# Two decoder layers on one core: the weight loads of the second layer's self-attention are issued two steps later in each pair of heads

## The reference

```python
def _L1_attn_ref(x, w_q, w_k, w_v, w_o):
    q = jnp.einsum('bsd,hqd->bhsq', x, w_q)
    k = jnp.einsum('bsd,hqd->bhsq', x, w_k)
    v = jnp.einsum('bsd,hvd->bhsv', x, w_v)
    scores = jnp.einsum('bhsq,bhtq->bhst', q, k)
    causal = jnp.triu(jnp.ones((s, s), dtype=bool), k=1)
    masked = jnp.where(causal, -jnp.inf, scores)
    weights = jax.nn.softmax(masked / jnp.sqrt(jnp.float32(dq)), axis=-1)
    out = jnp.einsum('bhst,bhtv->bhsv', weights, v)
    cat = out.transpose(0, 2, 1, 3).reshape(b, s, -1)
    return jnp.einsum('bsf,df->bsd', cat, w_o)
```

## Time and profile before

| | before |
|---|---|
| median of 3 runs | 3018.79 us (3016.57 to 3022.42) |
| the profiled execution, its own time | 3010.78 us |
| its span, first to last instruction | 3008.8 us |
| mean granted TensorE clock | 0.867 of full speed |

### The profile page before, as it was taken

The page is one execution under the profiler, slowest core; times in us unless marked ns, Lnnn a source line. Parts: engine busy times, 40 slices in busy tenths (PEclk is TensorE's granted clock), DMA queues, the critical chain, the costliest instruction groups (busy, mean ns, idle before and its releaser), DMA issues.

```text
span 3008.8 us, 50636 instructions
## 1 busy us (share of the span) xinstructions
PE 2276.8 (76%) x17470; PEld 1830.6 (61%) x17470; DVE 2175.1 (72%) x4246; ACT 1060.2 (35%) x2004; POOL 585.9 (19%) x666
## 2 busy tenths in 40 slices
PE   3667788868776877886877687888677777888875
PEld 3556666657465756664755565666565566666663
DVE  6765788866866578885776667888586666788767
ACT  2312444422432244442242224444224223444324
POOL 2111222212101122221101112222120102222220
PEclk8778899989777889998877789999877878999988
DMA  6001689840001078983000119897100014899600
GB/s 234 1 15 40 137 160 171 154 86 1 1 15 56 15 149 161 170 152 63 1 1 15 56 37 167 166 164 144 31 1 15 1 55 85 161 169 166 113 1 14
DMA packets 658407, 251.39 MB, mean 84 GB/s; under 512 B 613082, under 2 KB 633946, under 8 KB 657370
## 3 DMA queue, kind: packets, MB, share of 16 engines
q1 hardware_dynamic: 653978, 243.79, 41.4%
q10 hardware_dynamic: 4160, 4.19, 0.4%
HBM read 52.87 MB, written 10.49 MB: 21 GB/s over the span
## 4 chain that ended last, share of the span: by engine, by line
issue 38%; PE 23%; DVE 18%; DMA 11%; ACT 5%; POOL 4%; DVEq 1%; ACTq 0%; SPq 0%; POOLq 0%
DMA l_ptb<-l_phb 6%; PE ps L233 5%; PE ps L235 5%; PE ps L234 4%; DMA l_pts<-l_phs 4%; DVE nmax L1385 3%; PE ps L1289 1%; DVE l_k L1440 1%; DVE l_q L1444 1%; DVE l_phb L1391 1%; DVE l_phs L1391 1%; ACT l_q L1351 1%; PE ps L1271 1%; ACT xn L1347 1%; POOL d_pn L990 1%
## 5 line engine op out<-in xcount | busy, mean ns | idle before, releaser
L1385 DVE TENSOR_REDUCE nmax<-ps 128x1 f32<-128x1024 f32 (+7 forms) x512 | 383.3, 750 | 23.0 <-PE ps L1273 20.9
L1494 POOL CAST l_phb<-l_pb 128x1024 f16<-128x1024 f32 (+3 forms) x256 | 241.4, 943 | 654.1 <-ACT l_pb L1336 337.8
L1336 ACT ACTIVATE l_pb<-ps,nmax 128x1024 f32<-128x1024 f32 (+3 forms) x256 | 244.7, 956 | 283.5 <-DVE nmax L1385 282.7
L1271 PE MATMUL ps<-l_k,l_q 128*128 128x512 f32 (+3 forms) x768 | 319.1, 416 | 24.3 <-ACT l_ps L1336 23.9
L1391 DVE TENSOR_TENSOR l_phb<-l_pb,l_phb 128x1024 f16<-128x1024 f32 (+3 forms) x256 | 288.2, 1126 | 15.5 <-POOL l_phb L1494 13.4
L1272 PE MATMUL ps<-l_k,l_q 128*128 128x512 f32 (+3 forms) x768 | 270.1, 363 | 0.0
L1289 PE MATMUL ps<-l_v,l_ptb 128*128 128x64 f16 x4992 | 197.8, 197 | 34.2 <-DMA l_ptb<-l_phb 34.1
L1289 PEld LDWEIGHTS ps<-l_v,l_ptb 128*128 128x128 f16 x4992 | 177.1, 101 | 67.4 <-DMA l_ptb<-l_phb 41.1
L233 PE MATMUL ps<-xTh,l_w 128*128 128x512 f32 x256 | 123.1, 481 | 83.9 <-DVE l_q L1444 50.5
L1494 POOL CAST l_phs<-l_ps 128x128 f16<-128x128 f32 (+3 forms) x256 | 124.2, 485 | 319.1 <-DMA l_pts<-l_phs 169.6
L1271 PEld LDWEIGHTS ps<-l_k,l_q 128*128 128x128 f32 x768 | 156.0, 203 | 44.2 <-ACT l_ps L1336 29.8
(11 more groups left out here) (361 smaller groups left out, 6279.4 us busy)
## 6 DMA issues: line engine op xcount, KB each, us to landing
l_k<-xn SPq DMA_DIRECT2D x128, 256.0 KB, 4.1
l_w<-l_wqk_s SPq DMA_DIRECT2D x32, 512.0 KB, 4.8
l_wv<-l_wv_s SPq DMA_DIRECT2D x16, 512.0 KB, 6.0
xin<-in_x SPq DMA_DIRECT2D x4, 1024.0 KB, 5.5
m_w<-in_m_w SPq DMA_DIRECT2D x8, 512.0 KB, 4.4
m_w<-in_m_w SPq DMA_DIRECT2D x4, 1024.0 KB, 9.2
l_wo<-in_l_wo SPq DMA_DIRECT2D x16, 256.0 KB, 4.5
l_ptb<-l_phb SPq DMA_TRANSPOSE x256, 4.1
```

The source lines that it names most:

```text
L1271: pe.matmul(s[:, c0:c1], q, L["l_k1"][:, h, c0:c1], start=True, stop=False)
L1336: s.activation(l_numer(k)[:, 0:n], l_banks(k)[:, 0:n], ACT.Exp, bias=nmax[:, k % 4:k % 4 + 1], accum_out=lsum[:, h, k % NT:k % NT + 1]).th ...
L1385: v.tensor_reduce(nmax[:, k % 4:k % 4 + 1], l_banks(k)[:, 0:n], AX.X, ALU.max, negate=True).then_inc(q_["max"], 1)
L1494: g.tensor_copy(l_parts(k)[:, 0:cols], l_numer(k)[:, 0:cols]).then_inc(q_["hi"], 1)
```

## The change

The three conditions `k == 2` in `l_sp` become `k == 4`. The loads stand behind the block of head 0's key copies in the program, so at k = 4 the order on SP is: transpose of step 8, the two key copies of head 0, the weight loads, transpose of step 9. No other engine's program changes. What is loaded, from where and into which buffers stays as it was.

```diff
                 if j + 1 < HP and k == 10:
                     l_dup(sp, b, j + 1, 1)
-                if j + 2 < HP and k == 2:
+                if j + 2 < HP and k == 4:
                     sp.wait_ge(*lower(b, ("Q", j + 1 - 1, 1)))
                     l_load_w(sp, b, j + 2)
-                if j % 2 == 0 and j + 2 < HP and k == 2:
+                if j % 2 == 0 and j + 2 < HP and k == 4:
                     sp.wait_ge(*lower(b, ("V", j // 2, 3)))
                     l_load_wv(sp, b, j // 2 + 1)
-                if j % 2 == 1 and j >= 3 and k == 2:
+                if j % 2 == 1 and j >= 3 and k == 4:
                     sp.wait_ge(*lower(b, ("O", j // 2 - 1, 3)))
                     l_load_wo(sp, b, j // 2)
```

## The result

| | before | after |
|---|---|---|
| median of 4 runs | 3017.68 us (3004.45 to 3022.42) | 3066.17 us (3056.75 to 3074.18) |
| ratio to before | | 1.0168 (95% interval 1.0133 to 1.0202) |
| span of the profiled execution | 3008.8 us | 3054.8 us |
| mean granted TensorE clock of that execution | 0.867 | 0.861 |

The change makes the kernel slower by 48.5 us, or 1.7%. Forecast were +43 us and 3062 us. Of the 46.0 us between the two profiled spans, 42.7 us lie in the self-attention: from the first to the last `l_pv` of a batch it takes 9.6, 14.1, 9.1 and 9.9 us more. The other 3.3 us I did not trace to a place.

A forecast was written before the change was run, and what follows sets the result against it. Bound by a loop through all engines; DMA work delaying step 9's transpose, less 1.5 us slack per pair, gives 12.2 us per batch, 49 us in four, less 6 us for first pairs: +43 us, 3062 us, range 3018 to 3104 us.

The forecast's parts named there:

- What bounds the kernel: Whole kernel: bound by the length of a loop through all engines, no single one full; PE busy 76%, DVE 72%.
- Hole: SP idle for 3.3 us before step 8's transpose; DMA share 0.80 to 1.06 with loads, 0.47 without.
- dense stretch: SP from step 8's transpose past step 15's: issues within about 0.5 us of each other, DMA share 0.96 to 1.02.
- Leaving the hole is worth nothing, but 1.6 us per batch: Step 7's transpose lands 3.7 us sooner, priced at nothing; only pair 0 gains, 1.6 us per batch.
- the sum that I gave back: Pair 0 of each batch: PE's waits at two transposes shortly after the loads vanish, 6 us in all.
- Who waits and for how much: Behind step 9's later transpose POOL's rounding, then DVE, wait; 1.5 us per pair absorbed, 1.1 to 2.9 us left.
- SP's issue runs beside the DMA work and is not added: Before step 9's transpose: load issues add 0.7 us each on SP, 1.4 us for two, beside the DMA work.
- the slack that I had read: POOL's 0.9 us after step 13's rounding plus DVE's idle 0.6 us: 1.5 us per pair absorbed.
- the row's price: Loads in the dense stretch: 1 MB costs 4.4 us by the trace, against 2.4 us by the skill's ceiling.
- Full price: Dense stretch: no slack, SP, DVE and DMA each near full; 60 to 85 us slower, about 3090 us; chance 0.22.
- Absorbed: Dense stretch: loads slip between transposes, only SP's 1.4 us issue remains; no change, 3013 to 3025 us; chance 0.10.
- faster: `l_pv` at steps 8 to 10: waits in all pairs echo the hole's loads; 19 us less, 3000 us; chance 0.13.

The follow-up runs named there:

- the copies at k = 12: Kernel before with head 1's key copies issued at k = 12 instead of 10, except for the last pair: 3037.9 us, ratio 1.0058.
- the one that moves everything: Kernel before with loads at k = 0, head 0's key copies at k = 3 and head 1's at k = 12: 3022.2 us, ratio 1.0012.

## Why the prediction was right

The place, the direction and the order of the waits were right. The size came out right in part by luck: the waits cost less than forecast, and the clock, for which the prediction had no term, added an estimated 11 to 13 us.

*What bounds the kernel.* Hole and dense stretch are there, and the runs with other steps show that they decide: from k = 0 to k = 3 the time changes by 6 us, and between 3 and 4 by about 48 us.

*Leaving the hole is worth nothing, but 1.6 us per batch.* With the work taken away and the issues left at k = 2, the kernel gained 6 us, the sum that I gave back, 4 us of it in pair 0. With the change, step 7's transpose of pair 4 landed in 3.2 instead of 5.6 us, and nobody used it. In pair 0, from step 4 to step 8 of PE, the change gained 0.95 us per batch, not 1.6 us.

*Who waits and for how much.* The place and the order were right: step 9's landing, POOL's rounding, DVE's remainder. Both sizes were off in opposite directions. For pair 4, mean of the four batches, step 9's transpose landed 3.4 us later, counted from the issue of step 8's (11.25 against 7.85 us), and not 4.0 to 4.4 us. Of this, 1.7 us are a later issue and 1.7 us a longer landing. PE's step from `l_pv` 8 to `l_pv` 9 grew by 2.6 us, so about 0.8 us was absorbed and not 1.5 us. One sign came out short: the landing was to take 6 us or more from its issue and took 5.5 us, since half of the delay came ahead of the issue.

The pairs, from the end of `l_pv` of step 4 to that of the next pair, mean of four batches, in us:

| pair | 0 | 1 | 2 | 3 | 4 | 5 | 6 |
|---|---|---|---|---|---|---|---|
| loads | w, wv | w | w, wv | w, wo | w, wv | w, wo | none |
| predicted | 1.3 | 1.1 | 2.9 | 1.2 | 2.9 | 1.2 | 0 |
| measured | 2.1 | 1.5 | 2.1 | 2.2 | 2.5 | 1.1 | -0.8 |
| added time at the lower clock | 4.3 | 2.6 | 2.6 | 2.6 | 1.7 | 1.7 | -1.7 |

The sums are 10.6 and 10.7 us per batch. That they agree so well is luck: the spread over pairs is flatter than the bytes say, and at 0.24 us for each us at the lower clock 3.3 of the 10.7 us go with the clock. About 7.4 us are left for what the prediction described.

*SP's issue runs beside the DMA work and is not added.* Half right. It is not added: the loads without an issue on SP cost 59 us (though from another queue and a little earlier), the issues alone 19.5 us and both together 48.5 us. With ACT's queue, step 9's transpose of pair 4 took 4.1 us longer to land (7.9 against 3.8 us, mean of four), which is the work that I had read from the hole (4.4 us); behind SP's issues 1.7 us of it were left. But I put the issues at nothing if alone, as 1.4 us against 1.5 us of slack. They cost 19.5 us, as the slack that I had read belongs to step 9, and the one that SP's delay hits is step 10. This may be what flattens the table above, since a small load adds nearly an issue's time whatever it carries; no run shows it pair by pair.

*The figure of the Trainium skill.* By the ceiling of 435 GB/s (the Trainium skill, "DMA: Bandwidth & Descriptors", section Bandwidth) the change would have cost an estimated 7 us. The loads share the engines with transposes, and the busiest window of 8 us shown moves 251 GB/s; the row's price was the nearer one.

*The rivals.* Full price (60 to 85 us) was too much by 11.5 us or more for the change, though the loads from ACT's queue came near it with 59 us. Absorbed and faster are out: the interval of the ratio begins at 1.0133.

## What to carry to other kernels

A bulk load has no price of its own. It costs what it delays, so look along the queue for the stretch where the issuing sequencer stands idle and the DMA share has room once the load is taken out (here 0.47), and put the load there; here two steps later cost 1.7%, one step later nothing. Before moving a DMA ahead of others, price both what it adds to the DMA engines and what its issue adds to the sequencer, and look for the tight transfer behind it, which may be a different one for each. A move that empties one wait has to be followed to the buffers that the moved transfer still reads: the copies at k = 12 cleared 43 us of one wait and made 69 us of another. And read PE's busy time and the granted clock beside its idle time: a version can idle less and still be slower, as the one that moves everything shows.

## What was not expected of the hardware

- A second queue is no shelter. The same loads from ACT's queue made the kernel slower by 59 us instead of 48.5 us, and in pair 4 the issue of a transpose on SP took 5.38 us behind them (3.63 us in the change), against 1.3 to 1.4 us in the hole. The Trainium skill, "DMA: Bandwidth & Descriptors", section Issuing engines are not separate DMA queues, says that DMAs from several engines share the 16 DMA engines and that only issue time is saved; the trace agrees and shows that even the issue time of the other queue grows.
- A wait of PE can cost more than its length. The clock's falls lie behind PE's long waits (38 of 43 after), and after the fall shown above a matmul of 0.40 us takes 0.63 us.
- 48 issues of DMAs of 4 KB each, 0.8 to 1.2 us on SP, cost 19.5 us of the kernel's time by their place alone.
- The DMA share of the dense stretch was near 1.0 before, and yet 0.5 MB more went through it within 8 us, at 251 instead of 183 GB/s. A share near 1.0 is no proof that nothing more fits. Whether the time is lost to the packets' order or to their number was not tried.
